# Moving the first half of the next batch's projection into attention and layer one of a two-layer graph network

## The reference

```python
# layer one: graph attention, 8 heads of 64 units
feats = einsum('bnf,hfu->bhnu', X, W)
dense = leaky_relu(e_self[..., :, None] + e_neigh[..., None, :], 0.2) + NEG_BIG * (1 - A)
out   = relu(einsum('bhij,bhju->bhiu', softmax(dense), feats) + b)
x     = layernorm(x + out)
# layer two: mean over the neighbours
agg   = einsum('bij,bjf->bif', adj, x) / maximum(sum(adj, -1), 1e-6)
x     = layernorm(x + relu(einsum('bnf,of->bno', concatenate([x, agg], 2), W1)))
```

## Time and profile before

| | |
|---|---|
| time, median of 3 runs | 3591.5 us (3591.48 to 3596.26) |
| the profiled execution | 3595.57 us, span 3593.5 us |
| mean granted TensorE clock | 0.984 |
| PE / DVE / ACT / POOL busy | 3432.8 / 2486.6 / 1862.1 / 288.2 us |
| x tile load, adjacency tile load | 256 KB, 512 KB |

### The profile page before, as it was taken

One profiled execution on the slowest core, in us unless ns is written; L12 is line 12 of the kernel. 1 busy time (PEld: TensorE's weight loads), 2 busy tenths in 40 slices (PEclk: granted clock), 3 DMA queues, 4 the chain that ended last, 5 costly groups with the idle time before them and its releaser, 6 DMA issues.

```text
span 3593.5 us, 136396 instructions
## 1 busy us (share of the span) xinstructions
PE 3432.8 (96%) x59456; PEld 2906.5 (81%) x59456; DVE 2486.6 (69%) x4332; ACT 1862.1 (52%) x2313; POOL 288.2 (8%) x253
## 2 busy tenths in 40 slices
PE   6999999999999999999999999999999999999998
PEld 5969789697896978879788797887968779687896
DVE  5857668576685766858668586675867758677685
ACT  3636446364563645636456373563735537355463
POOL 0010200102010020100201001010020200202001
PEclk9999999999999999999999999999999999999999
DMA  4022030210302203022030210302103031130310
GB/s 144 34 71 69 14 107 33 77 63 14 113 27 77 68 10 111 27 77 68 13 113 22 80 66 19 108 21 83 62 26 104 19 105 41 31 102 15 100 35 24
DMA packets 79962, 214.90 MB, mean 60 GB/s; under 512 B 12672, under 2 KB 12672, under 8 KB 79360
## 3 DMA queue, kind: packets, MB, share of 16 engines
q1 hardware_dynamic: 79360, 205.82, 17.6%
HBM read 171.70 MB, written 34.08 MB: 57 GB/s over the span
## 4 chain that ended last, share of the span: by engine, by line
PE 85%; DVE 6%; POOL 4%; issue 4%; DMA 0%; ACT 0%; SPq 0%; POOLq 0%; DVEq 0%
PE six L817 72%; PE pair L817 9%; POOL x_parts L364 2%; POOL s_bc L358 2%; PE six L966 1%; PE six L854 1%; PE six L846 1%; DVE xs L708 1%; DVE stats L713 1%; DVE x_parts L571 0%; DVE feat L573 0%; DVE trl L582 0%; DVE adj_t L587 0%; DMA adj_nat<-in_adj_dram 0%; DVE s_bc L702 0%
## 5 line engine op out<-in xcount | busy, mean ns | idle before, releaser
L817 PE MATMUL six<-x_parts,mask 128*128 128x65 bf16 x16384 | 1546.9, 193 | 4.5 <-issue 3.2
L817 PE MATMUL six<-rest,mask 128*128 128x65 bf16 x16384 | 1546.9, 194 | 2.3 <-issue 1.7
L817 PE MATMUL six<-third,mask 128*128 128x65 bf16 x16384 | 1546.7, 193 | 1.2 <-issue 1.1
L817 PEld LDWEIGHTS six<-x_parts,mask 128*128 128x128 fp8e4 x16384 | 1536.9, 97 | 11.2 <-issue 11.0
L817 PEld LDWEIGHTS six<-third,mask 128*128 128x128 fp8e4 x16384 | 1536.1, 97 | 5.1 <-issue 4.1
L817 PEld LDWEIGHTS six<-rest,mask 128*128 128x128 fp8e4 x16384 | 1533.8, 97 | 1.3 <-issue 0.8
L416 ACT ACTIVATE step<-s_bc,n_step 128x1024 uint16<-128x1024 f32 x1024 | 1087.9, 1137 | 358.6 <-DVE mask L661 358.0
L661 DVE TENSOR_TENSOR mask<-adj_t,step 128x1024 uint16<-128x1024 uint16 x1024 | 652.5, 685 | 34.9 <-ACT step L416 33.0
L817 PE MATMUL six<-adj_t,x_parts 128*128 128x512 fp8e4 x1536 | 409.1, 387 | 47.6 <-POOL x_parts L364 31.0
L358 POOL TENSOR_TENSOR s_bc<-feat,rden 128x512 f32<-128x512 f32 x112 | 131.2, 1177 | 3077.6 <-DVE s_bc L702 3061.0
L817 PEld LDWEIGHTS six<-adj_t,x_parts 128*128 128x128 f16 x1536 | 142.5, 98 | 246.8 <-issue 105.5
(11 more groups left out here) (111 smaller groups left out, 4870.1 us busy)
## 6 DMA issues: line engine op xcount, KB each, us to landing
adj_nat<-in_adj_dram SPq DMA_DIRECT2D x128, 512.0 KB, 4.9
s_bc<-self_scores SPq DMA_DIRECT2D x128, 512.0 KB, 3.9
xs<-in_x_dram SPq DMA_DIRECT2D x128, 256.0 KB, 2.7
out_dram<-mask SPq DMA_DIRECT2D x128, 256.0 KB, 3.0
xs<-in_L_gnn_W_dram SPq DMA_DIRECT2D x1, 2048.0 KB, 12.6
feat<-in_L_gnn_W_dram SPq DMA_DIRECT2D x4, 256.0 KB, 4.4
self_scores<-sc_row SPq DMA_DIRECT2D x32, 16.0 KB
s_bc<-in_L_gnn_a_self_dram SPq DMA_DIRECT2D x1, 256.0 KB, 4.5
```

The lines of the kernel that those rows point to most:

```text
L817: return pe.matmul(o, l, r, start=start, stop=stop, skip_group_check=True)
```

## The change

The next batch's x is read a second time, apart from the copy in `xs` that the residual uses: tiles 0 to 3 into two of the adjacency slots (`lead_x`), tiles 4 to 7 into the step slots (`tail_x`). Tiles 0 to 3 are turned between the key tiles 10, 13, 18 and 21 of attention; scores(0) and features(0 to 3) of the next batch stand between the degree pass and the aggregate. Tiles 4 to 7 and adjacency tiles 0 to 5 are turned from t = 4 of layer two on. The head of the loop body then holds scores(1), features(4 to 7) and adjacency tiles 6 and 7. The maximum of the scores is taken in two halves. The adjacency isn't cast: its upper 16 bits are read as bfloat16, with a stride, and it has three slots. The diff, cut (renamed buffers, bank numbers of the small products and the prologue of ACT and DVE are left out):

```diff
+    ADJ_BANKS = (3, 7)
+    ADJ_SLOTS = 3
+    XT_BANKS = (6, 7, 6, 7, 0, 1, 0, 1)
+    FT_BANKS = (0, 1, 4, 5, 4, 5, 4, 5)
+    TURN_AT = (10, 13, 18, 21)
...
+        lead_x = adj_nat[:, 0:2].rearrange("p s (k d) -> p (s k) d", k=2)
+        adj_halves = [adj_nat[:, s].bitcast(BF16).rearrange("p (n z) -> p n z", z=2)[:, :, 1] for s in range(ADJ_SLOTS)]
+        tail_x = step[:, :, :].rearrange("p s n -> p (s n)").bitcast(F32).rearrange("p (t d) -> p t d", t=HALF)
...
@@ sync: before the loop @@
+            for t in range(HALF):
+                sp.dma_start(lead_x[:, t, :], x[0, t * P:(t + 1) * P, :]).then_inc(lead_in[t].sem, 16)
             sp.dma_start(a_bc[:, 0, :], rows(gat_self)).then_inc(w_in[1], 16)
...
+            def load_late_adj(b, t):
+                sp.wait_ge(at_ps.sem, at_ps.at(b, t - ADJ_SLOTS + 1))
+                load_adj(b, t)
...
+            load_adj(0, 2)
+            for t in range(HALF, T):
+                load_tail(0, t)
             sp.wait_ge(w1_ps, 2 * KC)
             for t in range(T):
                 load_x(0, t)
+            for s in range(2):
+                sp.wait_ge(xt_ps.sem, xt_ps.at(0, 2 * s + 2))
+                load_adj(0, s)
             store_scores(0, 0)
+            for t in range(3, T):
+                load_late_adj(0, t)
@@ sync: the loop @@
                 first_scores(b)
-                for t in range(2):
-                    sp.wait_ge(adj_cast.sem, adj_cast.at(b, T - 1 + t))
-                    load_adj(b + 1, t)
+                for s in range(2):
+                    sp.wait_ge(at_ps.sem, at_ps.at(b, T - 1 + s))
+                    load_lead(b + 1, 2 * s)
+                    load_lead(b + 1, 2 * s + 1)
+                load_adj(b + 1, 2)
                 for h in range(2, H):
                     load_scores(b, h)
+                    if h in (3, 4):
+                        s = h - 3
+                        sp.wait_ge(xt_ps.sem, xt_ps.at(b + 1, 2 * s + 2))
+                        load_adj(b + 1, s)
+                sp.wait_ge(masked.sem, masked.at(b, H * T))
+                for t in range(HALF, T):
+                    load_tail(b + 1, t)
+                store_scores(b + 1, 0)
                 for t in range(T):
                     sp.wait_ge(res_ok.sem, res_ok.at(b, t + 1))
                     load_x(b + 1, t)
                     if t >= 2:
                         store_y(b, t - 2)
+                    if t >= 4:
+                        load_late_adj(b + 1, t - 1)
                 store_y(b, T - 2)
                 store_y(b, T - 1)
+                load_late_adj(b + 1, T - 1)
@@ scalar @@
                     make_step(g)
+                    if more and g - 9 in TURN_AT:
+                        x_high(b + 1, TURN_AT.index(g - 9))
...
                     x1_parts_of(t)
-                    if t == 3:
+                    if more and t == 1:
+                        score_rows(b + 1, 0)
+                    if t == 5:
                         x1t_high(0)
...
                 for t in range(T):
+                    if more and t >= HALF + 1:
+                        act.wait_ge(o2_ps.sem, o2_ps.at(b, t))
+                        x_high(b + 1, t - 1)
                     if more and t == T - 1:
-                        cast_adj(b + 1, 0)
-                        cast_adj(b + 1, 1)
+                        act.wait_ge(o2_ps.sem, o2_ps.at(b, T))
+                        x_high(b + 1, T - 1)
                     by_degree(t)
@@ vector @@
+            def first_maximum(b):
+                dve.wait_ge(sc_f32.sem, sc_f32.at(b, 1))
+                dve.tensor_reduce(nmax16[:, 0:1], sc_row[:, 0:HALF * P], AX.X, ALU.max).then_inc(first_max.sem, 1)
+                dve.wait_ge(first_max.sem, first_max.at(b, 1))
+                dve.tensor_scalar(diag_first[:], ident[0:SC, 0:SC], nmax16[:, 0:1], None,
+                                  ALU.mult).then_inc(first_diag.sem, 1)
...
                     mask_word(g)
+                    if more and g - 7 in TURN_AT:
+                        x_low(b + 1, TURN_AT.index(g - 7))
...
                         last_head_rows(1, slice(QPB, T))
-                    if t == 4:
+                    if more and t == 1:
+                        first_maximum(b + 1)
+                    if more and 2 <= t < 2 + HALF:
+                        feature_rows(b + 1, t - 2)
+                    if t == 6:
                         x1t_low(0)
@@ vector: ln1 @@
                         ones_column(b + 1)
-                        adj_rows(b + 1, 0)
+                    if more and t >= HALF + 1:
+                        x_low(b + 1, t - 1)
+                        adj_rows(b + 1, t - HALF - 1)
                     dve.wait_ge(o2_sb.sem, o2_sb.at(b, t + 1))
...
                     if more and t == T - 1:
-                        x_low(b + 1, 0)
+                        x_low(b + 1, T - 1)
@@ vector: end of the body @@
                 if more:
-                    adj_rows(b + 1, 1)
-                    x_low(b + 1, 1)
+                    adj_rows(b + 1, 3)
                 ln1_end(T - 1)
+                if more:
+                    adj_rows(b + 1, 4)
+                    adj_rows(b + 1, 5)
@@ tensor @@
             def batch(b, more):
-                turn_x(b, 2)
-                turn_adj(b, 2)
-                features(0)
...
-                scores(1)
-                turn_adj(b, 5)
+                pe.wait_ge(sc_f32.sem, sc_f32.at(b, 1))
+                scores(b, 1)
+                features(b, 4)
                 pe.wait_ge(sc_f32.sem, sc_f32.at(b, 2))
...
                 ins.then_inc(nat_ps.sem, 1)
-                features(5)
                 pe.wait_ge(diag_ok.sem, diag_ok.at(b, 1))
                 mm(bank[6][:, 0:SC], ones16[:], diag16[:], True, True).then_inc(max_ps.sem, 1)
+                features(b, 5)
                 turn_adj(b, 6)
                 turn_adj(b, 7)
...
                     for jt in range(T):
+                        if more and h * T + jt in TURN_AT:
+                            turn_x(b + 1, TURN_AT.index(h * T + jt))
...
                         ins.then_inc(deg_ps.sem, 1)
+                if more:
+                    scores(b + 1, 0)
+                    features(b + 1, 0)
+                    features(b + 1, 1)
+                    pe.wait_ge(head_ok.sem, head_ok.at(b, H * GROUPS))
+                    features(b + 1, 2)
+                    features(b + 1, 3)
+                    pe.wait_ge(sc_f32.sem, sc_f32.at(b + 1, 1))
+                    pe.wait_ge(ft_sb.sem, ft_sb.at(b + 1, 2))
...
                     if jt == 1:
-                        pe.wait_ge(head_ok.sem, head_ok.at(b, H * GROUPS))
+                        if more:
+                            pe.wait_ge(ft_sb.sem, ft_sb.at(b + 1, HALF))
                         turn_x1(0)
...
                         turn_x1(t + 2)
+                    if more and t >= HALF:
+                        turn_adj(b + 1, t - HALF)
+                    if more and HALF <= t < T - 1:
+                        turn_x(b + 1, t)
+                    if more and t == T - 2:
+                        turn_x(b + 1, T - 1)
                 if more:
-                    turn_adj(b + 1, 0)
-                    turn_x(b + 1, 0)
-                    turn_x(b + 1, 1)
+                    turn_adj(b + 1, 4)
+                    turn_adj(b + 1, 5)
                     pe.wait_ge(o2_sb.sem, o2_sb.at(b, T))
-                    turn_adj(b + 1, 1)
                     pe.wait_ge(o_sum.sem, o_sum.at(b, T))
```

More of the change, by code:

```diff
@@ L388, in x_high, with score_rows @@
                 act.wait_ge(xt_ps.sem, xt_ps.at(b, t + 1))
[L389 to L399, removed]
+                copy(trh[:, :, col(t % HALF)],
+                     bank[XT_BANKS[t]][:].rearrange("p (k n) -> p k n", k=KC)).then_inc(xt_hi.sem, 1)
+            def score_rows(b, i):
+                act.wait_ge(sc_ps.sem, sc_ps.at(b, i + 1))
+                half = slice(i * HALF * P, (i + 1) * HALF * P)
+                copy(sc_row[:, half], bank[6][0:SC, :]).then_inc(sc_f32.sem, 1)
             def batch(b, more):
[L403 to L406, removed]
                 def make_step(g):
@@ L639, in batch @@
                 dve.tensor_scalar(ts_hi[:], ts[:], 0.0, None, ALU.max).then_inc(weights_in.sem, 1)
-                feature_rows(5)
+                feature_rows(b, 5)
+                adj_rows(b, 6)
                 for s in range(2):
@@ L805, in _ @@
             ones_column(0)
-            adj_rows(0, 0)
-            x_low(0, 0)
-            adj_rows(0, 1)
-            x_low(0, 1)
+            for t in range(HALF):
+                x_low(0, t)
+            for t in range(HALF):
+                feature_rows(0, t)
+            first_maximum(0)
+            for t in range(HALF, T):
+                x_low(0, t)
+            for t in range(6):
+                adj_rows(0, t)
             with dve.Fori(0, B - 1) as b:
@@ new lines, in features @@
+            def features(b, t):
```

(17 more changed lines are left out.)

174 lines of the change are left out of this document (63 added, 111 removed).

## The result

The kernel after takes 3605.21 us (median of 8 runs, 3602.66 to 3611.7), the kernel before beside it 3595.39 us (8 runs, 3591.48 to 3597.53). The ratio is 1.0037, with a 95% interval of 1.0028 to 1.0046: slower, by some 10 us.

A forecast was written before the change was run, and what follows sets the result against it. TensorE's own work bounds the kernel, plus some 160 us idle and low-clock losses. Terms -67.5 - 4.6 + 66.5 + 4.3 + 7.5 + 2.3 = +8.5 us on 3591.5 gave 3600 us, range 3570 to 3628.

The forecast's parts named there:

- Covering the layer norm: Between degree pass and aggregate: moved products hide layer norm one, gaining 4.5 us a batch in 15 batches, -67.5 us.
- Rival B: Aggregate: layer norm still late, TensorE waits and the clock falls again; +2.5 us per batch, 3637 us; chance 0.10.
- Turning in attention, no cast, layer two: Attention and layer two: moved turns, extra copies and loads, and strided transposes without the cast cost nothing.
- Rival D: Transposes of adj: strided reads cost double, 3655 us; chance 0.04.
- The turn of the batch: Loop end: turn_adj(5) waits for adj_rows(3), then the way back begins; +4.75 us in each of 14 turns, +66.5.
- Rival A: Way back to the loop's top: fetch overlaps the wait (3538 us, chance 0.12) or is shorter (3573 us, chance 0.11).
- The low clock: Behind the restart at the loop's top: loss of up to 1.7 us a turn stays as it is, 0.
- Rival C: Behind the restart: low clock lasts longer after a gap of 9 us; up to +24, 3624 us; chance 0.10.
- The last turn: Where the loop is left: no way back, but the wait for adj_rows(3) and low clock cost +4.3 us.
- The start: Before the loop: +2.8 us for lead loads ahead of the weights, +4.7 for the chains; +7.5 with the end.
- The last batch: Last batch: nothing covers the layer norm and x1t_low(0) comes later, so own(0) waits; +2.3 us.
- Rival E: Whole kernel: terms net to nothing, with the start at +2 and the residue at 0; 3591 to 3597 us; chance 0.20.

The follow-up runs named there:

- e9: Kernel before with every adj load inside the loop cut to 16 of 128 rows (output changed); 3587.76 us, ratio 0.9989.
- e10: e1 with every adj load inside the loop cut to 16 of 128 rows (output changed); 3648.27 us, ratio 1.0155 to the kernel before.
- e1: Kernel before with one wait added at the end of TensorE's loop body, for adj_rows(1) of the next batch; 3670.04 us, ratio 1.0197.
- e4: Kernel after with adjacency tile 5 turned at the head and without two waits ending TensorE's loop body; 3547.41 us, ratio 0.9862 to the kernel before.
- e6: Kernel after with adjacency tile 5 turned at the head and three batches in one loop body; 3497.57 us, ratio 0.9747 to the kernel before.
- e11: e6 with the four lead loads issued behind the load of the sage weights; 3507.16 us, ratio 0.9756 to the kernel before.
- e7: Kernel before with three batches in one loop body; 3557.45 us, ratio 0.9908.

## Why the prediction was right

The mechanism was right: the layer norm is covered, and what that gives is taken back at the turn of the batch by a late wait with the way back behind it. 3600 us was forecast, 3605.21 measured; of the 5.2 us between, 3.9 lie in the median from which I counted, 3591.5 then and 3595.39 beside the kernel after. Against their own medians it is +8.5 and +9.8 us. That these lie 1.3 us apart is partly luck. Over the run, the way back cost 8 us more than counted and the low clock some 10; the cover gave 7 us more than counted, the last turn 3, and 8 came from a stretch that is not placed. The terms:

- **Covering the layer norm**, -4.5 a batch: measured -5.0. Of the 41.67 us, 27.8 are the work counted before and 14.0 the moved products, so nothing is left to wait for; I had kept a residue of 0.2 and taken batch 7's loss for the mean. A tile of layer norm takes 3.2 us (3.1 to 3.3 predicted), and its tile 2 starts 6.6 us behind the degree pass where it was 3.9, so 2.7 late (2.5 predicted). Rival B fell.
- **The score row**, -0.31: gone, as said.
- **Turning in attention, no cast, layer two**, nothing: TensorE is busy 94.91 of 95.00 us there, and ACT's idle time before its steps went from 358.6 to 382.8, all of it waiting for masks. Eight strided transposes start 0.45 us apart as the contiguous ones do. Rival D fell.
- **The turn of the batch**, +4.75: measured 4.74 ahead of turn_adj(5) and 4.96 behind it, 9.70 lost in place of 4.33, so +5.4. I had the wait right and held the way back constant at 4.4. It isn't: it ran from 3.96 to 6.31. That is the term that was mis-sized, by 0.6 a turn or 8 us over the run. e9 and e10 show that loads beside the fetch lengthen it, and in the kernel after the same part of it is long, the time until the packet starts; with light loads that kernel was not run. Rival A, a fetch that overlaps the wait, falls with the gap and the packet behind turn_adj(5), and with e1, where wait and way back stand one behind the other. The Trainium skill ("Runtime: NRT & Kernel Launch", Instruction fetch mechanics) says that the sequencer must fetch a far branch target before it goes on. The traces agree: in the 14 turns of each of eight kernels, the one before, the one after and e1 to e4, e9, e10, TensorE restarts 1.5 to 1.7 us behind the end of an instruction packet. e4 adds that the sequencer may come to the branch while the array is still at work.
- **The low clock** behind the restart, granted 0.50 (the lower of the two levels, 1.2 GHz): 2.4 us lost in the turn of batch 6 where 1.7 were lost before, in the mean of 14 turns 2.2 against 1.9. Rival C named the right thing, but it is 0.3 a turn and not 1.7. turn_adj(5) itself runs at the low clock too, 0.4 more (1.01 us long, not 0.61). The prediction took the fall of the clock as a sign that transposes don't count as work. The traces don't show that. Here the clock fell at 1613.1, after TensorE had stood for 4.2 us, and in e6 it stays at 1.00 with transposes ahead of a wait of 1.75 us.
- **Together**: -5.0 and -0.3 on one side, +5.4, +0.3 and +0.4 on the other, +0.8 a period; the balance shows +0.24. The 0.6 between lie behind the restart (-0.8 in the table, where the score row and the clock add up to nothing), for the most part in the head of the batch. They are not placed; no experiment here splits that stretch.
- **The last turn**, predicted -4.8 + 4.3 = -0.5, measured -3.3. Of that, 1.8 are bookkeeping that I overlooked: the last attention has no turns of a next batch, while the first degree copy comes behind eight turns of batch 0 and four of batch 1. The other 1.0 is a gain that I had not counted, and it isn't placed.
- **The start**, +7.5: measured +7.7, of which 1.8 are those four turns. So 5.9, of which about 1 is for the loads (2.8 predicted) and the rest for the chains (4.7 predicted). The instant itself scatters by up to 3.3 us (e11), so no firmer split can be made, and the close agreement says little.
- **The last batch**, +2.3: measured +4.0. own(0) waits 2.01 us for x1t_l as foreseen. The waits for the parts of x1 ahead of it are 2.7 us, but they were 2.8 before. The rest is the low clock, 3.3 us lost in this stretch where it was 1.6. From the degree pass to neighbours(0), before and after:

```profile
3506.12:3538.86 32.74, 29.93 (x134) 13.90 (x133) 21.71 (x47) 17.51 (x29) 15.40 (x13) 0.95 0.00 1
```

```profile
3509.39:3546.25 36.86, 32.12 (x133) 14.76 (x133) 22.23 (x48) 17.56 (x29) 14.69 (x13) 0.91 0.00 1
```

Rival E (it nets to nothing) was the near miss: 0.6 us a turn less for the fetch would have given its time, though not by its own terms.

## What to carry to other kernels

Before work is moved to the end of a loop body, look at what its last wait waits for: everything after the branch stands behind that wait and the fetch, one behind the other, so here a wait of 4.7 us turned a gain of 1.5% into a loss of 0.4%. Turn the piece that waits longest at the head instead, and put several iterations in one body: the way back, invisible in a count of busy time, cost 3 to 6 us each. A wait taken from one engine's branch can bare the end of another engine's body, as in e4; look at both. And look twice at a gap that the list puts down to data: where it ends a fixed time after an instruction packet, it is the fetch.

## What the runs showed that I had not expected

- The way back has no fixed length: 4.05 to 4.87 us before, 3.96 to 6.31 after. What varies is the time until the instruction packet starts (1.2 us in the mean in e9, 2.4 in the kernel after); it is shorter when less is loaded beside it.
- Its cost depends on what it follows. Measured by leaving it out, it is 3.2 us a period in the kernel before and 5.7 in the kernel after.
- Without a wait at the body's end, TensorE's fetch lies over its own last work: the gap fell from 5.1 to 2.6 us. The list then puts it down to data, but the packet shows that it is still the fetch (e4). VectorE's end of the body then held TensorE up, and the time stayed.
- A short gap at the turn does not let the clock fall (1.75 us in e6), which made e6 better than forecast.
- ScalarE pays a way back as soon as three batches stand in its body (2.40 us in e7).
- The instant of the first degree copy differs by up to 3.3 us between executions with the same start, so a term of 3 us at the start can't be read from one of them.
